# Layer 3's mean squares of the keys as a pair of rounded matmuls, and the last values matmuls of a round behind its expert blocks

## The reference, cut to what matters

```python
def _unipool_layer(xt, router, W1, W2):
    logits = xt @ router
    probs = jax.nn.softmax(logits, axis=-1)
    w = jnp.max(probs, axis=-1)
    idx = jnp.argmax(probs, axis=-1)
    ...                       # for every expert i:
        h = jax.nn.silu(xt @ w1) @ w2
        sel = jnp.where(idx == i, w, 0.0)
        acc + sel[:, None] * h
```

```python
def rms_norm(x, w):
    rms = jnp.sqrt(jnp.mean(xf * xf, axis=-1, keepdims=True) + EPS)
    return (xf / rms * w)
kv = (ctx @ Wkv + bkv).reshape(B, Sc, 2, H, HD)
k = rms_norm(kv[:, :, 0], gk)
```

## Time and profile before

| | us |
|---|---|
| median of 3 runs | 2303.47 |
| lowest and highest | 2302.12, 2308.07 |
| profiled execution | 2300.54 |
| its span | 2298.8 |
| PE busy in it | 2092.4 (91%) |
| DVE busy | 1300.8 (57%) |
| ACT busy | 1456.4 (63%) |
| POOL busy | 229.1 (10%) |

### The profile page before, as it was taken

How to read it: one execution, slowest core, us unless ns; L and a number is a source line. 1 busy time by engine, 2 the same in 40 slices (tenths; PEclk the granted TensorE clock), 3 DMA queues, 4 the chain that set the end, 5 groups by cost and what they waited for, 6 DMA issues and landing times. The chain is left out here.

```text
span 2298.8 us, 42582 instructions
## 1 busy us (share of the span) xinstructions
PE 2092.4 (91%) x16862; PEld 1370.9 (60%) x16862; DVE 1300.8 (57%) x1812; ACT 1456.4 (63%) x1817; POOL 229.1 (10%) x302
## 2 busy tenths in 40 slices
PE   5878989989899599999859999998978999998999
PEld 3554856748568366666546666655645666665554
DVE  4653353343534677667477788754556766754233
ACT  2335456564565488888747888875437888885431
POOL 1006033150331300000010000000010000000000
PEclk9998989989899799999979999998988999998999
DMA  5888347374473877887156877721036788742000
GB/s 188 249 263 300 136 159 268 112 255 175 157 268 118 206 167 184 194 183 184 43 125 153 198 180 184 182 66 49 0 83 157 183 189 189 184 100 75 2 6 7
DMA packets 119594, 351.74 MB, mean 153 GB/s; under 512 B 20128, under 2 KB 54814, under 8 KB 118910
## 3 DMA queue, kind: packets, MB, share of 16 engines
q1 hardware_dynamic: 105614, 321.36, 51.4%
q0 software_dynamic: 13776, 27.54, 3.9%
HBM read 257.58 MB, written 91.23 MB: 152 GB/s over the span
## 5 line engine op out<-in xcount | busy, mean ns | idle before, releaser
L969 ACT ACTIVATE a_probs<-a_score 128x1200 f32<-128x1200 f32 x768 | 858.0, 1170 | 167.0 <-PE a_score L880 167.0
L880 PE MATMUL a_score<-a_qstack,a_kstack 128*128 128x400 f32 x2304 | 551.9, 372 | 27.3 <-issue 26.7
L880 PEld LDWEIGHTS a_score<-a_qstack,a_kstack 128*128 128x128 f32 x2304 | 380.1, 190 | 197.1 <-issue 149.2
L842 PE MATMUL a_numer<-a_probs,a_v 128*18 128x200 f32 (+1 forms) x9216 | 471.6, 335 | 0.0
L842 PEld LDWEIGHTS a_numer<-a_probs,a_v 128*18 128x18 f32 (+1 forms) x9216 | 228.5, 97 | 184.8 <-issue 88.6
L1030 DVE TENSOR_TENSOR a_kstack<-a_kraw,a_kstack 64x2888 fp32r<-64x2888 f32 x96 | 303.8, 3164 | 5.1 <-ACT a_kstack L936 1.8
L1038 DVE TENSOR_TENSOR a_qstack<-a_qrep,k_groupmask 128x1600 fp32r<-128x1600 f32 x48 | 87.5, 1824 | 128.0 <-PE a_score L880 127.5
L1025 DVE CAST a_kstack<-a_kraw 128x2888 fp32r<-128x2888 f32 x90 | 149.8, 1665 | 10.7 <-DVE a_own L1086 8.8
L2166 ACT ACTIVATE f_hidden<-f_ph,f_b 128x400 f32<-128x400 f32 x128 | 76.0, 594 | 88.4 <-PE f_ph L2090 80.8
L1755 PEld LDWEIGHTS f0r_ph<-f0r_xsT,f0r_w 128*128 128x128 f32 x896 | 115.3, 193 | 27.4 <-DVE f0r_w L1902 5.5
L1755 PE MATMUL f0r_ph<-f0r_xsT,f0r_w 128*128 128x128 f32 x896 | 119.9, 277 | 4.9 <-DVE f0r_w L1902 2.1
(11 more groups left out here) (359 smaller groups left out, 2716.1 us busy)
## 6 DMA issues: line engine op xcount, KB each, us to landing
a_kraw<-keys SPq DMA_DIRECT2D x384, 361.0 KB, 7.0
values<-kv_vst SPq DMA_DIRECT2D x32, 1296.0 KB, 5.4
a_v<-values SPq DMA_DIRECT2D x48, 864.0 KB, 5.8
keys<-kv_made SPq DMA_DIRECT2D x48, 722.0 KB, 7.2
l0a_ctxT<-in_ctxT SPq DMA_DIRECT2D x16, 722.0 KB, 7.5
kv_ctxT<-in_ctxT SPq DMA_DIRECT2D x16, 722.0 KB, 7.0
l0a_ctx<-in_ctx SPq DMA_DIRECT2D x16, 704.0 KB
l0a_mask<-in_mask_BxSxS_ik SPq DMA_DIRECT2D x16, 564.1 KB
```

Of the source, the lines that this page charges most:

```text
L842: last = pe.matmul(numer[32 * g:32 * g + PC, p * 2 * SQ:(p + 1) * 2 * SQ], v[0:rows(t), j, t, (2 * g + p) * PC:(2 * g + p + 1) * PC], prob ...
L880: last = pe.matmul(to, kstack[:, j, g * SK + t * 128:g * SK + (t + 1) * 128], qstack[:, j, g * GH:(g + 1) * GH, :], start=True, stop=not s ...
L969: act.activation(probs[:, n % NP, :].rearrange("p (g q) -> p g q", g=SPAN), slot_ps[:, n % 2, :, 0:GQ], ACT.Exp, scale=HSCALE).then_inc(ex ...
```

## The change

1. The squares of a chunk are parted by DVE (`squares_dve`): `khigh` is the square rounded to fp32r, `klow` the rest, also rounded. PE multiplies both by the rounded block average and adds them up in the bank: two fp32r matmuls for one full-precision one. `khigh` and `klow` exist once, so DVE waits for the last chunk's `n_full` ahead of a cast.
2. In rounds 1 to 3 the last 8 of the 24 late values tiles, in round 4 the last 12, are taken out of the blocks and stand behind the last block on PE and ACT, ahead of the late keys; ACT's table load follows them.
3. On DVE, the calls of `squares_dve` stand ahead of the normals of each batch. The maximum of `late[0]`'s layer 2 moves to the next round's start; in round 1 the second early batch's normals go ahead of the first weights copy and `turned_in(0)`, in the others only its squares do.

```diff
+LATER, LAST_LATER = 8, 12
...
+        self.klow = o.sb("klow", [128, 512], F32R)
+        self.khigh = o.sb("khigh", [128, 512], F32R)
+        self.average = o.sb("average", [128, 128], F32R)
...
-            pe.wait_ge(self.squared, 3 * b + ci + 1)
-            pe.matmul(bank[:, 0:m], self.k.blockavg[:, :], self.ksq[:, a:a + m], start=True, stop=True).then_inc(self.n_full, 1)
+            pe.wait_ge(self.averaged, 1)
+            pe.wait_ge(self.low_ready, 3 * b + ci + 1)
+            pe.matmul(bank[:, 0:m], self.average[:, :], self.khigh[:, 0:m], start=True, stop=False)
+            pe.matmul(bank[:, 0:m], self.average[:, :], self.klow[:, 0:m], start=False, stop=True).then_inc(self.n_full, 1)
...
+    def squares_dve(self, dve, b):
+
+        for ci in range(3):
+            a, m = KCHUNKS[ci]
+            n = 3 * b + ci + 1
+            square = self.ksq[:, a:a + m]
+            dve.wait_ge(self.squared, n)
+            if n > 1:
+                dve.wait_ge(self.n_full, n - 1)
+            dve.tensor_copy(self.khigh[:, 0:m], square).then_inc(self.high_ready, 1)
+            dve.wait_ge(self.high_ready, n)
+            dve.tensor_tensor(self.klow[:, 0:m], square, self.khigh[:, 0:m].bitcast(F32),
+                              ALU.subtract).then_inc(self.low_ready, 1)
...
+        between = len(late) * KT - (LATER if more else LAST_LATER)
...
-                    if s < len(late) * KT:
+                    if s < between:
                         values_between(s)
...
             groups(pe, group)
+            for u in range(between, len(late) * KT):
+                values_between(u)
...
             groups(act, group)
+            for u in range(between, len(late) * KT):
+                maker.values_act(act, late[u // KT], u % KT, spare[u % 2])
...
             if layer:
+                maker.largest_dve(dve, mine[0] - 2, 2)
...
+            maker.squares_dve(dve, early[0])
             maker.normals_dve(dve, early[0], banks)
             for n in (1, 2):
                 maker.largest_dve(dve, early[0], n)
+            maker.squares_dve(dve, early[1])
+            if layer == 0:
+                maker.normals_dve(dve, early[1], banks)
             weigh(0, 0)
             turned_in(0)
-            maker.normals_dve(dve, early[1], banks)
+            if layer:
+                maker.normals_dve(dve, early[1], banks)
...
+            maker.squares_dve(dve, late[0])
             maker.normals_dve(dve, late[0], banks)
             if more:
                 scale(0)
-                for n in (1, 2):
-                    maker.largest_dve(dve, late[0], n)
+                maker.largest_dve(dve, late[0], 1)
+                maker.squares_dve(dve, late[1])
                 maker.normals_dve(dve, late[1], banks, (0,))
...
                 scale(0)
+                maker.squares_dve(dve, late[1])
                 maker.normals_dve(dve, late[1], banks, (0, 1))
```

More of the change, by code:

```diff
@@ L500, in __init__ @@
         self.inverted, self.normal = o.sems("inverted normal")
+        self.high_ready, self.low_ready, self.averaged = o.sems("high_ready low_ready averaged")
     def loads(self, sp):
@@ L1858, in _ @@
         def _(dve):
+            if layer == 0:
+                dve.tensor_copy(maker.average[:, :], k.blockavg[:, :]).then_inc(maker.averaged, 1)
             dve.sem_inc(up_full, 1)
```

## The result

The changed kernel takes 2312.08 us, the median of 10 runs (2309.03 to 2316.72); the kernel before takes 2301.73 in 10 runs beside it. The ratio is 1.0057, 95% interval 1.0046 to 1.0068: **slower by 0.57%**. That share of the time before is 13.1 us, while the two medians lie 10.4 us apart (0.45%); the two figures are not computed in the same way, and I use the ratio to compare kernels with one another. The forecast was 18.7 us and a time of 2322, in a range of 2304 to 2334.

A forecast was written before the change was run, and what follows sets the result against it. PE was taken to bound the expert blocks, PE and DVE the round ends, POOL's gather level. Rounds of -0.3, 4.25, 4.8 and 8.4 gave 17.2, plus 1.5 for slow casts: +18.7 us, 2322 at the median, range 2304 to 2334.

The forecast's parts named there:

- case 3: Rival, no change: blocks at PE's 1.78, ACT absorbs late table load and turn-back wait, POOL costs nothing; 2307, chance 0.20.
- Case 1: The forecast itself: 18.7 us slower, 2322 at the median, 2313 to 2333 from its bounds, chance 0.60.
- No gain booked for the saved PE work: Keys passes: the 18 us of PE work saved turns into waits for DVE, through a loop of 1.89 us per chunk.
- The sign that PE's busy time would fall by 18 us: Sign of being right: rounded pairs lower PE's busy time by about 18 us while the kernel's time goes up.
- Blocks without values: Expert blocks: 1.97 us each, 8.33 per group, saving 1.83; late keys 1.8 later, 2.8 in round 4; 1.8 each meant wrong.
- Late table load: Start of the late keys: ACT loads behind the last values copy, so its first square comes about 0.9 us later.
- Tails of rounds 2 and 3: Late keys to round end: PE ends the keys at 22.3 instead of 20.8, picks 0.1 later still; +1.6 us.
- Tail of round 4: DVE's queue delays the second batch's squares to 15.9, last scale 33.7 instead of 29.5: +4.2; no DVE gap from 13 on.
- Starts: Round starts: -3.0 us in round 1 from normals going ahead, +0.85 in round 2, +1.4 each in rounds 3 and 4.
- DVE's casts beside POOL, +1.5 us: Casts beside POOL's scatter and gather: one in three on the waiting path, 0.28 us longer each, adding 1.5.
- nobody is waiting for it then: Behind the blocks: the gather starts 3.7 and 5.5 us earlier, but nothing waits for it, so no gain was booked.
- The faster rival: Saved PE work shows if cast and subtraction take under 0.6 us instead of 1.2; 2285, chance 0.10.

The follow-up runs named there:

- Two slots: The whole change with khigh and klow in two slots each, the cast waiting for the pair before the last one; ratio 1.0008 to the kernel before.
- the pair alone: The whole change with the values matmuls back in their blocks, rounded pair and DVE's new order kept; ratio 1.0063 to the kernel before.
- the move alone: The whole change with one full-precision average per chunk, no cast or subtraction, values behind the blocks and DVE's new order kept; ratio 0.9994 to the kernel before.
- The full-precision run: The whole change with the last round's two late batches averaged in full precision, without casts and subtractions; ratio 1.0041 to the kernel before.
- the four parts together: The change with double khigh and klow, last round's late batches in full precision, table load behind the last silu, early casts behind the maxima; 0.9982 to before, median 2294.4.
- short maxima: Values in their blocks, rounded pair kept, the second early batches' maxima reading 32 of 1444 columns; ratio 1.0055 to the kernel before.
- the parts-together kernel: The change with double khigh and klow, last round's late batches in full precision, table load behind last silu, early casts ahead of the maxima; ratio 1.0027 to before.
- values behind and values back: Both with double khigh/klow, last late batches in full precision: values behind blocks, table load behind last silu, 0.9982; values in blocks, maxima moved, 1.0013; to before.

## Why the prediction was right, and where its sizes were off

The direction and the mechanism held, and the time lies in the range of 2304 to 2334: the loop over one slot takes what the pair saves on PE, and DVE's queue ends the last round later. The forecast difference was too large (18.7, against 10.4 between the medians or 13.1 by the ratio). The range held because it reaches over case 3 as well. Case 1's own span was given as 2313 to 2333, and the measured 2312.08 lies just below it; the bounds named beside it (7 less, 9 more around 2322) in fact give 2315 to 2331.

The runs of the parts show where the excess was. I had priced the move and the new order at +5.2 us (late starts of 1.8, 1.8, 1.8 and 2.8, round 1's -3.0), and alone they measured -1.4 us (interval -4 to +1.4). The pair on top of them, from 0.9994 to 1.0057, is 14.5 us, where the rest of my sum had 13.5, the late table load included. So the loss from the pair was sized about right, and the price of the move was not. Term by term:

- **No gain booked for the saved PE work:** right. The loop was forecast at 1.89 us and is 2.11. Its cast and subtraction took their 0.43 and 0.69; the pair took 0.54 instead of 0.46, from the subtraction's end to PE 0.15 instead of 0.06, and from the pair's end to the next cast 0.27. Two slots took the loop out and gave 0.5%. The sign that PE's busy time would fall by 18 us was wrong: over the four rounds it fell by 4.7, from 531.1 to 526.4. Two things pull against each other: in the pair alone it is 519.0, in the move alone 536.1. A pair is 0.32 us cheaper and not 0.40, and a value behind the blocks keeps PE busy for 0.73 us instead of 0.65; by my estimate that is 3 of the 5 us that the move adds (36 values at 0.08 us), and the rest is open.
- **Blocks without values:** the mis-sized term that matters most. I took 8.33 us a group from three intervals of the earlier trace rows; it is 7.66, close to the bound of PE alone, 7.57, which I had set aside. Those intervals were of a round's last group, whose third block waited for a weight copy, and I took it to stand for the others. Blocks without values at 1.8 us were one of my signs of being wrong, and it came: (7.66 - 0.45) / 4 = 1.80. That gives 2.5 us a group instead of 1.83. Values behind the blocks cost 0.73 instead of 0.69. Net, the late keys came 1.0, 0.7 and 0.4 us later in rounds 2 to 4, where I had 1.8, 1.8 and 2.8. The two measured terms give 0.8, 0.8 and 1.2; what took 0.8 off in round 4 is open.
- **Late table load:** the first square 0.9 us later, as forecast. Loading behind the last silu gives back 0.6 to 0.8 of it.
- **Tails of rounds 2 and 3:** forecast +1.6 us, measured +2.2 and +2.9 to the last scale. Averages at 4.01, 6.12 and 8.09 (3.9, 5.8, 7.5 forecast), the next batch at 10.97 (10.3): the longer loop, three times.
- **Tail of round 4:** forecast +4.2, the second batch's squares at 15.9 and the end at 33.7; measured 16.2, 34.4 and +4.9. The full-precision run shows that it is the pair's. The sign that DVE would run without a gap from 13 us on did not come: its second and third cast there waited 1.11 and 1.45 us for pairs, the loop again.
- **Starts:** +1.4 us in rounds 3 and 4, measured 1.4 and 1.4. In round 2 I booked +0.85 and it was -0.6: before, a DMA was waited for there, and it came at another time. In round 1 the first down comes 25.4 us behind the early keys and came 28.5 behind: -3.1, with -3.0 forecast. 2.3 us of that round went into the later start of its early keys, which is in other profiles too, with and without the pair.
- **DVE's casts beside POOL, +1.5 us:** not there. The 32 long casts take 436 ns in the mean, 9 more than the median copy of the same size: 0.3 us in all. 26 of them overlap an instruction of POOL, and two are long, 0.57 and 0.62 us. The weight copies, from which I had taken my share, did behave otherwise: in the change's profile 21 of 112 overlap POOL, all with its direct stores of the blocks' rows (`outputs<-f0r_xs`), and all 21 are long, 0.60 to 0.72 us. One of each kind, from the change's timeline, each 0.27 us behind the start of POOL's:

```profile
391.85 0.76 POOL L1691 DMA_DIRECT2D outputs<-f0r_xs  x1 [21.27 <-DVE f0r_xs L1936]
392.12 0.71 DVE L1930 COPY f0r_w<-f_w 128x512 f32 x1 [0.56 <-issue]
...
452.08 1.00 POOL L1695 DMA_INDIRECT f_rows<-outputs,f0r_slot  x1 [0.30 <-issue]
452.35 0.43 DVE L655 CAST kv_khigh<-kv_ksq 128x512 fp32r<-128x512 f32 x1 [4.71 <-ACT kv_ksq L593]
```

22 of the 26 casts stand beside POOL's indirect scatter or gather issues instead, and the step that failed was to carry the copies' share over to them. Here the Trainium skill ("SBUF — State Buffer", Who interferes with whom) speaks of an exclusion of a VectorE copy or cast that uses both ports and a GpSimd instruction. The copies agree with it; by it alone the casts would be late as well, and hardly any was. With two slots and the other parts more casts are long: 10 of 28 in the four parts together, at 0.47 to 0.59 us, 6 of them beside the gather's issues; what makes the difference is not shown.
- **The gather, "nobody is waiting for it then":** true of the change, where no scale waits for it, but it hid from me what the move was for. Before, five scales waited for the gather, 7.8 us in all, and with the values back in their blocks the first scale waits for it again as soon as DVE gets there early (0.88 us with two slots, 2.21 with short maxima). I booked the move's price and not this gain.

The rivals: no change (2307) was 5 us off, the forecast 10, so its number was the nearer one. The direction is clear of noise all the same. That rival had right that the blocks go at PE's pace and that POOL costs nothing, which are two of its three pieces; the third, ACT absorbing the late table load, did not come. The faster rival named its deciding point as cast and subtraction under 0.6 us. With two slots the loop is out of the way by another route, and then ACT allows only 0.3 us a pass.

What stays open: whether the pair pays at all beside a kernel with the other parts and full-precision averages; why seven of twelve executions of the parts-together kernel take 2304 us and more, and how much of the 7 us between values behind and values back belongs to the move itself, how much to the maxima.

## What to carry to other kernels

A cheaper instruction that needs a helper on another engine buys a loop: add up helper, hand-over, instruction and hand-back over the number of slots, and compare that with the work between two uses. If it is longer, a second slot is the first thing to try and the next engine's busy share in that stretch is the ceiling. When work is moved behind a stage, ask what other queues do in the meantime; it may be cover for them, and then its price alone says little of its worth beside another change. And place helper work in an in-order queue by what stands ahead of it, above all a step that waits for a DMA.

## What the runs showed of the hardware that I had not expected

In a rounded pair of 512 columns whose first matmul waited for DVE, the second starts 0.31 us behind the first (all 23 such pairs of the change's profile lie at 0.305 to 0.31), and the next matmul 0.23 us behind the second (453.65, 453.96, 454.19); the first of a pair is the dearer one. From the second's start to DVE's next cast, which waits for it, it is 0.50 us. ACT writes squares as rounded numbers at the same 0.61 us for 420 elements as in full precision, so a rounding there costs no time in this kernel:

```profile
353.02 0.61 ACT L592 ACTIVATE kv_ksq<-f0r_py,kv_cols 128x420 fp32r<-128x420 f32 x1
```
